# Second scan layer: every state in SBUF, the last columns kept by a DMA, four weight banks in PSUM

## The chip, the cores and the metric

The kernel runs on one core of a Trainium2 chip. The core has a matrix engine (TensorE, "PE" in the profile), a vector engine (VectorE, "DVE"), a scalar engine (ScalarE, "ACT"), GpSimd ("POOL") and SyncE ("SP"), which here only issues DMAs. The engines work through their own queues in order and meet at semaphores. SBUF is the on-chip memory that all of them read and write; PSUM is the small second memory, in eight banks of 512 float32 per partition, which TensorE writes and which VectorE and ScalarE also read and write. GpSimd and the DMAs reach SBUF only here. The metric is the time of one execution on the device, in microseconds.

## The reference

Four layers run one after the other on an image batch of 4 x 96 x 56 x 56: attention, a selective scan in eight directions, window attention, and a selective scan in four directions with a convolutional tail. The change is in the last of them, the second scan layer. Cut to what matters, its scan is

```python
def step(hc, inp):                        # hc: one state per channel d and state index n
    u_t, d_t, B_t, C_t = inp
    hc = hc * jnp.exp(d_t[..., None] * A[None]) + (d_t * u_t)[..., None] * B_t[:, :, None, :]
    return (hc, jnp.einsum('bkdn,bkn->bkd', hc, C_t))
```

with 192 channels, 16 state indices n, 4 directions and a sequence of 56*56 = 3136 positions. For each position the state decays, takes an input, and is summed over n with the weights C.

## The kernel before

All is float32. Two images are worked on together (a "pair"), 64 channels of each on the 128 partitions, so 192 channels are three slices c = 0, 1, 2. The layer runs for two pairs, one after the other. For a pair, `scans` goes over 4 directions times 7 tiles of T = 448 positions, in all 28 **blocks** q. A block has 16 **groups**, one for each n; a group g has three scans (g, c), numbered u = 3g + c. So a pair has 448 groups and 1344 scans. The same function serves both scan layers; `ratio` is true in the second one, and only its branches matter here.

For one group the engines do the following, each in its own queue:

- ACT makes the decay of each scan (L1319, an Exp into `Ar`, a ring of NA = 6) and a weight (L1329, a Tanh into a PSUM bank, a ring of NW = 3 banks, `weight_bank`). The function that orders them makes weight u+2 and decay u+4 in iteration u. Weight u may only be written when the scan that used its bank is over, three scans back (`weight_before`).
- POOL forms du * B for all three slices (`input1`, L1579, into `Tr`, two groups ahead), and multiplies states by C (`project` of POOL, L1595).
- DVE turns a weight into an input in its bank (`input2`, L1454) and runs the scan (`scan`, L1478) with Ar and that bank as its inputs.
- Of every second group (the even ones, `on_dve(g)` = 1 - g % 2) DVE also multiplies slice 0 by C (`project` of DVE, L1485). The state of that slice is written to PSUM bank 3 (`HB`), all other states to SBUF (`Hr`, a ring of NH = 3 groups). POOL's `project` takes the two slices that are left of an even group, and all three of an odd one.
- PE adds the products to a PSUM bank per slice (L1205).
- ACT copies the last column of each state to `st`, from SBUF (`keep_sbuf`, L1340) and from PSUM (`keep_psum`, L1335); 16 groups later `seed` (L1352) puts it in front of the next tile's decays, as the start of that scan. `seed` of group g+1 waits for the last scan of group g-1.
- SP loads B and C of each group, spread over partitions, into `BC` (`spread`, L1638, two DMAs a group, four groups ahead).

DVE's queue for an even group g is: input2, scan (g,0), input2, scan (g,1), project (g,0), input2, scan (g,2). POOL's queue for each group g is: project of g-1, input1 of g+2.

Beside this the next block is prepared: POOL gathers its inputs (L1556, one slice in each of the groups r = 1, 2, 3 of the block) and forms du (L1562, r = 11, 12, 13, the last one when ACT has read `delta` at the start of r = 14); ACT loads another function table and back, with a logarithm between them (r = 9); DVE does `one_less` (L1411, once a block, after scan (10,0)) and three cumulative sums (L1420: after scan (11,2), after (13,0), and after (14,1) just ahead of that group's project).

Of the kernel before, what the change touches and what calls it, by code (L numbers as in the profile page):

```python
# [1028 lines left out]
def scans(chip, K, D, lay, pair, xc, yacc, bcd, S):  # L1029
# [6 lines left out]
    def on_dve(g):  # L1036
        return (1 if ratio else 2) - g % 2
# [4 lines left out]
    def kept_before(g):  # L1042
        return g + (g + 1) // 2 if ratio else 2 * g

    FIRST_SB = 0 if ratio else 1
    NBS = 5 if ratio else 6
    HB, YB, XB = (3, 4, 7) if ratio else (2, 4, 7)
    NA, NW = (6, 3) if ratio else (2, 0)
    TW, TP = T + 1, T + 4
# [19 lines left out]
    with ExitStack() as ctx:  # L1069
# [31 lines left out]
        w_done, t2_done = sems("w_done"), sems("t2_done")  # L1101
        st_done, y_free, merged = sems("st_done"), sems("y_free"), sems("merged")

        def weight_bank(u):
# [16 lines left out]
        def state_at(g, c, first):  # L1121
            return PS[:, HB + c, first:TW] if c < on_dve(g) else Hr[:, g % NH, c - FIRST_SB, first:TW]

# [107 lines left out]
        def act(e):  # L1231
# [110 lines left out]
            def seed(g):  # L1342
# [3 lines left out]
                if g >= ring:  # L1346
                    e.wait_ge(s_done, 3 * (g - ring + 1))
                if q % NT:
                    e.wait_ge(st_done, kept_before(g - 15))
                else:  # L1350
                    e.wait_ge(zeroed, 1)
# [20 lines left out]
            for u in range(-2, NU):  # L1372
# [12 lines left out]
                if c == 0 and g + 1 < NG:  # L1385
                    seed(g + 1)
                if c == 2:
                    keep_sbuf(g)
# [4 lines left out]
                if q + 1 < NQS:  # L1393
                    prepare(q + 1, s)
                if c == 1 and ratio and on_dve(g):
                    keep_psum(g)
            for c in range(3):
                merge(NQS - 1, c)

        def dve(e):  # L1400
# [56 lines left out]
            def scan(g, c):  # L1457
# [10 lines left out]
                else:  # L1468
                    e.wait_ge(t_done, g + 1)
                if c < on_dve(g) and g:  # L1470
                    e.wait_ge(h_done, products_before(g))
                    last = g - 2 if ratio else g - 1
                    if last >= 0:
                        e.wait_ge(st_done, kept_before(last) + 1)
                elif c >= on_dve(g) and g >= NH:
                    e.wait_ge(hp_done, g - NH + 1)
                    e.wait_ge(st_done, kept_before(g - NH + 1))
# [135 lines left out]
        def sp(e):  # L1613
# [14 lines left out]
            def spread(g):  # L1628
# [8 lines left out]
                for m in range(2):  # L1637
                    e.dma_start(BC[64 * m:64 * m + 64, g % NBS],  # L1638
                                bcd[q % 2, 16 * m + nn:16 * m + nn + 1].broadcast_to([64, 2, T])).then_inc(bc_ld[g % NBS], 16)

            put_rows(0)
            for g in range(min(NBS - 1, NG)):
                spread(g)
            for g in range(NG):
# [5 lines left out]
                if g + NBS - 1 < NG:  # L1650
                    spread(g + NBS - 1)

        chip.stage(pe, act, dve, pool, sp)
# [1384 lines left out]
```

## Time and profile before

| | us |
|---|---|
| median of 3 runs | 15305.25 (15288.34 to 15307.01) |
| the profiled execution | 15302.04 |
| its span, first to last instruction | 15299.9 |
| DVE busy over the span | 14142.6 |
| POOL busy over the span | 12419.2 |
| ACT busy over the span | 11996.8 |

The span and the time differ by 2.1 us, so the trace holds the whole of the time. The busy times are over all four layers; what bounds the second scan layer has to be read from its own stretch, which lies at 9838 to 12205 us for the first pair and at 12632 to 15002 us for the second. Instructions of one engine overlap a little in the records: the next starts some 0.09 us before the end shown for the one ahead, so a cost in a queue is read from start to start.

### The profile page before, as it was taken

What the parts mean: (1) busy time and instruction counts of PE and PEld (TensorE: products, weight loads), DVE (VectorE), ACT (ScalarE), POOL (GpSimd) and SP (SyncE); (2) the same over time, 40 slices, a digit from 0 to 9 for tenths busy, and PEclk for the clock granted to TensorE, in tenths of its full rate; (3) what the DMA queues carried; (4) which work ended last, traced back from release to release, by engine and by line L of the source; (5) the groups of instructions that cost most, each with busy time, mean ns of one, the idle gap of its engine ahead of it and who ended that gap; (6) DMA issues with size and microseconds to landing.
All of it is one profiled execution on the core that took longest, in us unless ns stands there. A gap on an engine that the chain in (4) does not pass through costs nothing. (4 is left out here: it accounts for less than half of the span.)

```text
span 15299.9 us, 186073 instructions
## 1 busy us (share of the span) xinstructions
PE 13023.2 (85%) x37976; PEld 5684.4 (37%) x37976; DVE 14142.6 (92%) x19364; ACT 11996.8 (78%) x26319; POOL 12419.2 (81%) x6712
## 2 busy tenths in 40 slices
PE   9999799999999889999999979877777677777776
PEld 3333244444444334444444435433333233333333
DVE  7778699999999989999999988899999979999998
ACT  6777678788888767878888855699889858988996
POOL 1111599999999879999999972599999859999996
PEclk9999899999999999999999989999999889999988
DMA  2110244444444334444444432233333213332331
GB/s 39 30 26 17 69 121 121 122 121 120 119 120 120 107 108 122 120 122 120 120 120 120 120 105 66 61 90 89 89 88 89 83 46 89 89 89 87 89 88 45
DMA packets 543491, 1416.85 MB, mean 93 GB/s; under 512 B 134802, under 2 KB 191274, under 8 KB 538778
## 3 DMA queue, kind: packets, MB, share of 16 engines
q1 hardware_dynamic: 542342, 1404.94, 32.5%
q14 instruction: 845, 6.92, 0.2%
q8 instruction: 304, 4.98, 0.1%
HBM read 1323.37 MB, written 58.28 MB: 90 GB/s over the span
## 5 line engine op out<-in xcount | busy, mean ns | idle before, releaser
L1205 PE MATMUL PS<-Hc,ident 128*128 128x448 f32 x16128 | 7100.2, 580 | 1452.2 <-POOL Hc L1595 1389.6
L1579 POOL TENSOR_TENSOR Tr<-du,BC 128x1344 f32<-128x1344 f32 x2684 | 6886.8, 2566 | 0.0
L1205 PEld LDWEIGHTS PS<-Hc,ident 128*128 128x128 f32 x16128 | 3091.0, 200 | 5346.3 <-issue 2793.0
L1595 POOL TENSOR_TENSOR Hc<-Hr,BC 128x896 f32<-128x896 f32 (+2 forms) x2688 | 4409.1, 1640 | 199.4 <-DVE Hr L1478 193.3
L1319 ACT ACTIVATE PS<-dl,A 128x448 f32<-128x448 f32 x5376 | 3402.4, 633 | 1009.5 <-DVE Hr L1478 689.3
L1478 DVE TENSOR_TENSOR_SCAN Hr<-PS,Tr 128x449 f32<-128x449 f32 x2688 | 2895.4, 1077 | 4.1 <-ACT PS L1319 3.4
L1478 DVE TENSOR_TENSOR_SCAN PS<-PS,Tr 128x449 f32<-128x449 f32 x2688 | 2837.1, 1077 | 60.8 <-ACT PS L1319 57.9
L1478 DVE TENSOR_TENSOR_SCAN Hr<-Ar,PS 128x449 f32<-128x449 f32 x2240 | 2417.2, 1079 | 0.0
L1329 ACT ACTIVATE PS<-cs,lneps,A 128x448 f32<-128x448 f32 x2688 | 1928.5, 719 | 138.2 <-DVE Hr L1478 75.0
L1485 DVE TENSOR_TENSOR Hc<-PS,BC 128x448 f32<-128x448 f32 x3136 | 1823.5, 605 | 0.0
L1454 DVE SCALAR_TENSOR_TENSOR PS<-PS,Tr 128x448 f32<-128x448 f32 x2688 | 1651.7, 614 | 154.9 <-ACT PS L1329 146.3
L1319 ACT ACTIVATE Ar<-dl,A 128x448 f32<-128x448 f32 x2688 | 1764.8, 657 | 0.0
L528 DVE TENSOR_REDUCE mx<-PS 128x1 f32<-128x448 f32 (+1 forms) x2100 | 1204.5, 618 | 328.0 <-PE PS L308 327.0
L494 ACT ACTIVATE Pr<-PS 128x896 f32<-128x896 f32 (+1 forms) x1092 | 936.1, 885 | 403.5 <-PE PS L326 388.3
L620 POOL TENSOR_TENSOR ost<-ost,rb 96x448 f32<-96x448 f32 x84 | 95.0, 1131 | 1313.9 <-DMA rb<-rows 1313.9
L1214 PE MATMUL PS<-yacc,ident 128*128 128x448 f32 (+15 forms) x1320 | 761.0, 685 | 11.3 <-ACT yacc L1310 10.3
L308 PE MATMUL PS<-K,Q 96*128 96x448 bf16 (+1 forms) x2100 | 741.2, 360 | 5.8 <-DMA K<-part 5.5
L326 PE MATMUL PS<-Q,K 99*128 99x448 bf16 (+1 forms) x2100 | 734.0, 358 | 1.4 <-ACT Q L455 0.8
L1335 ACT ACTIVATE st<-PS 128x2 f32<-128x2 f32 (+1 forms) x2240 | 360.6, 161 | 415.8 <-DVE Hc L1485 410.9
L1157 PE MATMUL PS<-dl,ident 128*128 128x448 f32 x984 | 490.7, 582 | 169.7 <-issue 169.7
L1340 ACT ACTIVATE st<-Hr 128x2 f32<-128x2 f32 (+2 forms) x2688 | 519.2, 193 | 76.0 <-DVE Hr L1478 11.0
L340 PE MATMUL PS<-Pr,V 128*32 128x448 f32 (+1 forms) x4200 | 561.7, 551 | 0.0
(288 smaller groups left out, 15088.0 us busy)
## 6 DMA issues: line engine op xcount, KB each, us to landing
BC<-bcscratch SPq DMA_DIRECT2D x5376, 224.0 KB, 3.6
zscratch<-zst SPq DMA_DIRECT2D x84, 224.0 KB, 1.9
bcscratch<-rows SPq DMA_DIRECT2D x336, 56.0 KB, 1.7
z<-zscratch SPq DMA_DIRECT2D x28, 672.0 KB, 4.9
rb<-rows SPq DMA_DIRECT2D x12, 1176.0 KB, 7.1
xg<-mid SPq DMA_DIRECT2D x12, 1176.0 KB, 8.1
xr<-mid SPq DMA_DIRECT2D x56, 168.0 KB, 2.7
rl<-rows SPq DMA_DIRECT2D x56, 168.0 KB, 3.3
```

Source lines behind the costliest of these rows:

```text
L308: e.matmul(PS[0:qn, bank("max", v), 0:T], Q[s][0:96, q0:q0 + qn], KK[s][0:96, i * T:i * T + T], start=True, stop=True).then_inc(full, 1)
L494: e.activation(Pr[0:kn, n % NPR, 0:nt, :], PS[0:kn, 2 * (n % 2):2 * (n % 2) + nt, 0:T], ACT.Exp, scale=scale).then_inc(s_exp, 1)
L528: e.tensor_reduce(mx[0:qn, t, i:i + 1], PS[0:qn, bank("max", v), 0:T], AX.X, ALU.max).then_inc(drained("max", v)[0], 1)
L1205: e.matmul(PS[:, YB + c, 0:T], K["ident"][:], Hc[:, g % NHC, c, :], start=False, stop=(nn == 15)).then_inc(y_done, 1)
L1214: e.matmul(view(PS[:, YB + c, :], ro, rd), K["ident"][:], view(yacc, c * n + off, dims), start=(i == 0), stop=False)
L1319: e.activation(decay_at(u, 1), dl[:, q % 2, c, :], ACT.Exp, scale=A[:, q // NT, c, nn:nn + 1]).then_inc(a_done, 1)
L1329: e.activation(PS[:, weight_bank(u), 1:TW], cs[:, q % 2, c, :], ACT.Tanh, scale=A2[:, q // NT, c, nn:nn + 1], bias=K["lneps"][:]).then_inc ...
L1454: e.scalar_tensor_tensor(out=p, in0=p, scalar=1.0, in1=Tr[:, g % NTR, c, :], op0=ALU.add, op1=ALU.mult).then_inc(t2_done, 1)
L1478: e.tensor_tensor_scan(state_at(g, c, 0), decay_at(u, 0), input_at(g, c), 1.0 if ratio else 0.0, ALU.mult, ALU.add).then_inc(s_done, 1)
L1485: e.tensor_tensor(Hc[:, g % NHC, c, :], state_at(g, c, 1), BC[:, g % NBS, 1, :], ALU.mult).then_inc(h_done, 1)
L1579: e.tensor_tensor(Tr[:, g % NTR] if ratio else Tr[:, g % NTR, :, 1:TW], du[:, q % 2], b, ALU.mult).then_inc(t_done, 1)
L1595: e.tensor_tensor(Hc[:, g % NHC, m:3], Hr[:, g % NH, m - FIRST_SB:3 - FIRST_SB, 1:TW], c_, ALU.mult).then_inc(hp_done, 1)
```

## The change

In the second scan layer only:

- All scans write their states to SBUF (`Hr`); DVE's `project` of an even group, slice 0, reads its state from there. PSUM bank 3 becomes free and joins the ring of weights (NW = 4).
- ACT's two copies of last columns go. SP issues one DMA per group for it (`keep`), from the last column of the three states to `st`, when the group's last scan is done. It stands behind the `spread` of the same iteration.
- `seed` waits for that DMA of 16 groups before. The first scan of a group waits, before it overwrites a slot of `Hr`, for the DMA and for both engines' products of three groups before.

```diff
@@ kept_before, the rings
-        return g + (g + 1) // 2 if ratio else 2 * g
+        return 2 * g
...
-    NA, NW = (6, 3) if ratio else (2, 0)
+    NA, NW = (6, 4) if ratio else (2, 0)
@@ state_at
-            return PS[:, HB + c, first:TW] if c < on_dve(g) else Hr[:, g % NH, c - FIRST_SB, first:TW]
+            return PS[:, HB + c, first:TW] if c < on_dve(g) and not ratio else Hr[:, g % NH, c - FIRST_SB, first:TW]
@@ act: seed
-                if q % NT:
+                if q % NT and ratio:
+                    e.wait_ge(st_out[(g - 16) % NH], 16 * ((g - 16) // NH + 1))
+                elif q % NT:
                     e.wait_ge(st_done, kept_before(g - 15))
@@ act: the loop over u
-                if c == 2:
+                if c == 2 and not ratio:
                     keep_sbuf(g)
...
-                if c == 1 and ratio and on_dve(g):
-                    keep_psum(g)
@@ dve: scan
-                if c < on_dve(g) and g:
+                if ratio:
+                    if g >= NH and c == 0:
+                        e.wait_ge(h_done, products_before(g - NH + 1))
+                        e.wait_ge(hp_done, g - NH + 1)
+                        e.wait_ge(st_out[g % NH], 16 * (g // NH))
+                elif c < on_dve(g) and g:
                     e.wait_ge(h_done, products_before(g))
-                    last = g - 2 if ratio else g - 1
-                    if last >= 0:
-                        e.wait_ge(st_done, kept_before(last) + 1)
+                    e.wait_ge(st_done, kept_before(g - 1) + 1)
@@ sp
+            def keep(g):
+                e.wait_ge(s_done, 3 * g + 3)
+                e.dma_start(st[:, g % 16, :], Hr[:, g % NH, :, T], allow_slow_non_contiguous=True).then_inc(st_out[g % NH], 16)
...
                     spread(g + NBS - 1)
+                if ratio:
+                    keep(g)
```

On DVE, in the program order of one even and one odd group (the engine's scan is listed under the name SCALAR_TENSOR_TENSOR; `Hc` are the products, `BC` the spread B and C), before:

```order
L1454 SCALAR_TENSOR_TENSOR PS<-PS,Tr 128x448
L1478 SCALAR_TENSOR_TENSOR PS<-Ar,PS 128x449
L1454 SCALAR_TENSOR_TENSOR PS<-PS,Tr 128x448
L1478 SCALAR_TENSOR_TENSOR Hr<-Ar,PS 128x449
L1485 TENSOR_TENSOR Hc<-PS,BC 128x448
L1454 SCALAR_TENSOR_TENSOR PS<-PS,Tr 128x448
L1478 SCALAR_TENSOR_TENSOR Hr<-Ar,PS 128x449
L1454 SCALAR_TENSOR_TENSOR PS<-PS,Tr 128x448
L1478 SCALAR_TENSOR_TENSOR Hr<-Ar,PS 128x449
L1454 SCALAR_TENSOR_TENSOR PS<-PS,Tr 128x448
L1478 SCALAR_TENSOR_TENSOR Hr<-Ar,PS 128x449
L1454 SCALAR_TENSOR_TENSOR PS<-PS,Tr 128x448
```

and after:

```order
L1455 SCALAR_TENSOR_TENSOR PS<-PS,Tr 128x448
L1482 SCALAR_TENSOR_TENSOR Hr<-Ar,PS 128x449
L1455 SCALAR_TENSOR_TENSOR PS<-PS,Tr 128x448
L1482 SCALAR_TENSOR_TENSOR Hr<-Ar,PS 128x449
L1489 TENSOR_TENSOR Hc<-Hr,BC 128x448
L1455 SCALAR_TENSOR_TENSOR PS<-PS,Tr 128x448
L1482 SCALAR_TENSOR_TENSOR Hr<-Ar,PS 128x449
L1455 SCALAR_TENSOR_TENSOR PS<-PS,Tr 128x448
L1482 SCALAR_TENSOR_TENSOR Hr<-Ar,PS 128x449
L1455 SCALAR_TENSOR_TENSOR PS<-PS,Tr 128x448
L1482 SCALAR_TENSOR_TENSOR Hr<-Ar,PS 128x449
L1455 SCALAR_TENSOR_TENSOR PS<-PS,Tr 128x448
```

The number of instructions is the same. The project's first input has moved from PSUM to SBUF, so that both of its inputs (Hr and BC) are now in SBUF; that of each scan's output has moved too.

On ACT, two groups in a block (L1329 or L1330 is a weight, L1319 or L1320 a decay, L1352 or L1355 the seed, L1282 or L1283 the copy of `delta` at r = 12, 13 or 14), before:

```order
L1329 ACTIVATE PS<-cs,lneps,A_464 128x448
L1319 ACTIVATE Ar<-dl,A 128x448
L1340 ACTIVATE st<-Hr 128x3
L1329 ACTIVATE PS<-cs,lneps,A_464 128x448
L1319 ACTIVATE Ar<-dl,A 128x448
L1352 ACTIVATE Ar<-still 128x3
L1329 ACTIVATE PS<-cs,lneps,A_464 128x448
L1319 ACTIVATE Ar<-dl,A 128x448
L1335 ACTIVATE st<-PS 128x1
L1329 ACTIVATE PS<-cs,lneps,A_464 128x448
L1319 ACTIVATE Ar<-dl,A 128x448
L1340 ACTIVATE st<-Hr 128x2
```

and after:

```order
L1330 ACTIVATE PS<-cs,lneps,A_470 128x448
L1320 ACTIVATE Ar<-dl,A 128x448
L1330 ACTIVATE PS<-cs,lneps,A_470 128x448
L1320 ACTIVATE Ar<-dl,A 128x448
L1355 ACTIVATE Ar<-still 128x3
L1330 ACTIVATE PS<-cs,lneps,A_470 128x448
L1320 ACTIVATE Ar<-dl,A 128x448
L1330 ACTIVATE PS<-cs,lneps,A_470 128x448
L1320 ACTIVATE Ar<-dl,A 128x448
```

The three copies to `st` of two groups have gone; all else stands in its old order.

On SP, the start of the layer's loop for a pair (L1626 or L1630 writes B and C of a block out, L1618 and L1619 or their successors load the next direction's weights), before:

```order
L1626 DMA bcscratch<-rows 32x448 x2
L1638 DMA BC<-bcscratch 64x896 x8
L1618 DMA xp<-in_l3xp 128x228
L1619 DMA dw<-in_l3dw 12x384
L1638 DMA BC<-bcscratch 64x896 x8
L1626 DMA bcscratch<-rows 32x448 x2
```

and after:

```order
L1630 DMA bcscratch<-rows 32x448 x2
L1642 DMA BC<-bcscratch 64x896 x8
L1622 DMA xp<-in_l3xp 128x228
L1623 DMA dw<-in_l3dw 12x384
L1642 DMA BC<-bcscratch 64x896 x2
L1648 DMA st<-Hr 128x3x1
L1642 DMA BC<-bcscratch 64x896 x2
L1648 DMA st<-Hr 128x3x1
L1642 DMA BC<-bcscratch 64x896 x2
```

The loads of a block stood together; now every pair of loads is followed by the DMA of a group's last columns, 128 partitions x 3 single elements, 896 such DMAs in all.

## Rows read from the trace of the kernel before

**Rows 1.** Busy time of each engine in the first pair of the layer

```profile
9840.00:12205.00 2365.00, 1785.31 (x3820) 760.51 (x3820) 2290.03 (x3017) 2127.03 (x4310) 2215.51 (x1056) 0.91 0.31 88
```

**Rows 2.** One_less, once a block, in two stretches: min/median/max ns, first and last start

```profile
L1411 DVE TENSOR_SCALAR w<-du x12: 1539/1541/1542, 9972.5 to 10899.1; 128x1344 f32<-128x1344 f32 x12
...
L1411 DVE TENSOR_SCALAR w<-du x12: 1539/1540/1543, 11071.3 to 12009.8; 128x1344 f32<-128x1344 f32 x12
```

**Rows 3.** Groups in 11100 to 12100: count, busy us, mean ns, idle before

```profile
L1454 DVE SCALAR_TENSOR_TENSOR PS<-PS,Tr 128x448 f32<-128x448 f32 x564 | 346.6, 615 | 37.6 <-ACT PS L1329 35.8
L1556 POOL COPY xs<-xc 128x448 f32<-128x448 f32 x36 | 36.6, 1017 | 0.0
L1420 DVE TENSOR_TENSOR_SCAN cs<-one,cs,PS 128x448 f32<-128x448 f32 x30 | 33.7, 1122 | 0.0
L1562 POOL TENSOR_TENSOR du<-dl,xs 128x448 f32<-128x448 f32 x33 | 32.3, 978 | 33.6 <-ACT dl L1282 33.6
```

**Rows 4.** Who waited for whom in the same stretch: us, times, longest

```profile
ACT st L1335 <- DVE Hc L1485: 37.8, 46, 1.4
POOL Hc L1595 <- DVE Hr L1478: 22.6, 11, 2.1
```

**Rows 5.** POOL's gather in the first half of the first pair

```profile
L1556 POOL COPY xs<-xc x36: 549/559/565, 9932.9 to 10869.8; 128x448 f32<-128x448 f32 x36
```

**Rows 6.** Timeline of DVE in a plain stretch: start us, length us

```profile
13507.08 0.60 DVE L1485 TENSOR_TENSOR Hc<-PS,BC 128x448 f32<-128x448 f32 x1
13507.59 0.62 DVE L1454 SCALAR_TENSOR_TENSOR PS<-PS,Tr 128x448 f32<-128x448 f32 x1
13508.13 1.08 DVE L1478 TENSOR_TENSOR_SCAN Hr<-Ar,PS 128x449 f32<-128x449 f32 x1
...
13509.64 1.08 DVE L1478 TENSOR_TENSOR_SCAN Hr<-Ar,PS 128x449 f32<-128x449 f32 x1
...
13514.19 1.09 DVE L1478 TENSOR_TENSOR_SCAN PS<-Ar,PS 128x449 f32<-128x449 f32 x1
```

**Rows 7.** Timeline of POOL at the same place

```profile
13503.03 2.56 POOL L1579 TENSOR_TENSOR Tr<-du,BC 128x1344 f32<-128x1344 f32 x1
13505.55 2.56 POOL L1595 TENSOR_TENSOR Hc<-Hr,BC 128x1344 f32<-128x1344 f32 x1
13508.07 2.56 POOL L1579 TENSOR_TENSOR Tr<-du,BC 128x1344 f32<-128x1344 f32 x1
13510.60 1.77 POOL L1595 TENSOR_TENSOR Hc<-Hr,BC 128x896 f32<-128x896 f32 x1
13512.33 2.56 POOL L1579 TENSOR_TENSOR Tr<-du,BC 128x1344 f32<-128x1344 f32 x1
```

**Rows 8.** Timeline at one place of the first pair's tail

```profile
12285.21 1.51 POOL L1773 TENSOR_TENSOR yacc<-yacc,z 128x448 f32<-128x448 f32 x1
...
12285.77 1.44 DVE L775 SCALAR_TENSOR_TENSOR acc<-pad,cw,acc 128x448 f32<-128x448 f32 x1
```

**Rows 9.** The same view, 1.5 us later

```profile
12286.68 1.51 POOL L1773 TENSOR_TENSOR yacc<-yacc,z 128x448 f32<-128x448 f32 x1
```

**Rows 10.** Instructions by line: ns min/median/max, first and last start

```profile
L775 DVE SCALAR_TENSOR_TENSOR PS<-pad,cw,PS x624: 687/690/692, 1709.3 to 15277.7; 128x448 f32<-128x448 f32 x156
L775 DVE SCALAR_TENSOR_TENSOR acc<-pad,cw,acc x128: 683/685/1621, 12284.3 to 15163.2; 128x448 f32<-128x448 f32 x128
...
L1684 DVE TENSOR_TENSOR ysum<-ysum,yacc x28: 624/626/1443, 5324.1 to 15075.1; 128x448 f32<-128x448 f32 x28
...
L1485 DVE TENSOR_TENSOR Hc<-PS,BC x3136: 594/606/618, 1811.7 to 14996.1; 128x448 f32<-128x448 f32 x196
...
L1773 POOL TENSOR_TENSOR yacc<-yacc,z x84: 1125/1137/1647, 5347.7 to 15141.9; 128x448 f32<-128x448 f32 x84
```

**Rows 11.** DMA issues: count, KB each, us from issue to landing

```profile
BC<-bcscratch SPq DMA_DIRECT2D x5376, 224.0 KB, 3.6
...
bn<-in_bn SPq DMA_DIRECT2D x4, 6.0 KB, 1.7
```

More of the change, by code:

```diff
@@ L1102, in scans @@
         st_done, y_free, merged = sems("st_done"), sems("y_free"), sems("merged")
+        st_out = [sems("st_out") for _ in range(NH)]
         def weight_bank(u):
@@ L1651, in sp @@
                     spread(g + NBS - 1)
+                if ratio:
+                    keep(g)
+            if ratio:
+                for i in range(NH):
+                    e.wait_ge(st_out[i], 16 * len(range(i, NG, NH)))
         chip.stage(pe, act, dve, pool, sp)
```

## The prediction

> **What bounds the kernel now.** I read the trace's stretch of this layer first. In the first pair DVE is busy for 2290 of 2365 us, POOL for 2216, ACT for 2127 [rows 1]. So DVE sets the time, POOL is 3% behind it, and ACT has a tenth to spare. The length of a block comes from an instruction that stands once in it: twelve starts in 926.6 us make 84.24 us a block in the first half of a pair, where the gathers are short, and 938.5 / 11 = 85.32 us in the second half, where they are long [rows 2].
>
> Then DVE's own work in a block, from start to start. A scan with its input2 takes 1.51 us (13508.13 to 13509.64) and the project 0.51 (13507.08 to 13507.59) [rows 6]. one_less is 1.54 and a cumulative sum 1.12 long [rows 2, 3], each less the overlap of 0.09. That is 48 x 1.51 + 8 x 0.51 + 1.45 + 3 x 1.03 = **81.2 us**. DVE is idle for the rest, 3.0 us of a block in the first half and 4.1 in the second. The wait that ends last there is for ACT's weight: 35.8 of 37.6 us of idle time before input2 in 1000 us [rows 3]. ACT is late although it has time to spare, because it may not run ahead by more than three banks, and stands itself behind the copies of last columns, which wait for DVE (37.8 us in 1000 before the copy from PSUM alone) [rows 4].
>
> POOL's queue runs without a break in a plain stretch: starts at 3.03, 5.55, 8.07, 10.60 and 12.33 us [rows 7], so 2.52 for input1, 2.52 for an odd group's project, 1.73 for an even one's, 9.29 us for two groups, where DVE needs 6 x 1.51 + 0.51 = 9.57. POOL is idle before a project only 11 times in 1000 us [rows 4]. It is as good as always in the middle of an instruction when DVE comes to its project.
>
> **What the change removes.** ACT loses three copies in two groups and the waits before them, and may be a fourth bank ahead. I take all of DVE's wait for weights as gone: -3.0 us a block in the first half, -4.1 in the second. The bounds are nothing and this.
>
> **What it adds on DVE.** DVE's project now reads Hr and BC, both in SBUF; before, one input was in PSUM. This form with PSUM took 594 to 618 ns in all its 3136 uses, POOL busy or not [rows 10]. A project with both inputs in SBUF isn't in the trace, but other DVE instructions of that kind and size are: L1684 takes 624 ns at least and 1443 at most, L775 with acc 683 and 1621, whereas L775 on PSUM never leaves 687 to 692 [rows 10]. The timeline shows what makes the difference. POOL's L1773 runs to 12286.72, DVE's L775 starts at 12285.77 and ends only at 12287.21, 0.49 us after POOL [rows 8]. POOL's next one starts at 12286.68 and is 1.51 long instead of 1.13 [rows 8 to 10]; POOL goes on 0.38 us late. So a DVE instruction with two inputs in SBUF waits for the end of POOL's instruction, POOL is then held for 0.38, and DVE goes on 0.45 after POOL's changeover (0.49, plus 0.05 and less 0.09 of overlaps).
>
> How long this wait can be is not in the rows: POOL's instructions there are 1.13 us long, here up to 2.57. With the longest surplus of rows 8 as a cap (1.44 - 0.63 = 0.81 us) it costs less, with the end of POOL's instruction as the only limit it can be 2.5. I take the latter, since the end of DVE follows POOL's end and no fixed time. The Trainium skill (SBUF — State Buffer, section "SBUF: two separate sides") says that a DVE instruction with two SBUF inputs and a GpSimd instruction which reads SBUF take a shared port pair by an exclusive lock, and that the loser blocks for the whole instruction. By that page the wait has no cap either, and its sum is the one below; by the cap it would be 15,302.
>
> **The walk through a block**, with both queues side by side:
> - *Plain pairs (r = 0, 6, 8).* From one changeover, DVE is back at its project after 0.45 + 9.07 = 9.52. POOL needs 0.38 + 2.52 (input1) + 1.73 + 2.52 + 2.52 = 9.67 to the end of the odd group's project. DVE waits 0.16 and goes in between project and input1.
> - *r = 2 and r = 4.* POOL has one gather more (0.52 from start to start, later 0.97; 0.04 less than the lengths in [rows 3, 5]) and then two: 0.68 and 1.19 in the first half, 1.13 and 2.09 in the second.
> - *r = 10.* one_less stands ahead of it: DVE comes 1.45 later, 1.30 after the changeover, and meets input1: it waits the rest, 1.22. After that POOL is idle until scan (10,2) is over.
> - *r = 12.* POOL took 1.73 + 2.52 + 0.94 for group 11 against DVE's 4.53, so its project of group 11 ends 3.31 after scan (11,2), and input1 5.83. DVE, with a cumulative sum, comes at 1.03 + 3.02 = 4.06: 1.78.
> - *r = 14.* POOL has waited for ACT's `delta` with its third du (33.6 us in 1000 [rows 3]) and is late with its project: DVE, again behind a sum, waits 0.43.
>
> Together 5.8 us a block in the first half and 7.1 in the second. A block becomes 81.2 + 5.8 - 8 x 0.06 = **86.5** (before 84.24) and 81.2 + 7.1 - 0.5 = **87.8** (before 85.32). That is +2.3 and +2.5, 28 blocks of each: +134 us. In the first block of a pair POOL isn't late yet, DVE meets input1 instead of the gap before it, and it costs 7.5 more, twice: +15.
>
> **The rest.** States of slice 0 into SBUF instead of PSUM: a scan takes 1.08 into SBUF and 1.09 into PSUM [rows 6], 0. The wait of scan (g,0) for both products and the DMA of g-3 is covered by two groups, 9 us. SP's DMA waits for the scans of g; behind it stands the spread of g+5, which waits for POOL's project of g anyway and is read 10 us later. A small DMA lands in 1.7 us, the large ones in 3.6 [rows 11]. One whose last dimension is strided becomes one descriptor per element by the Trainium skill (DMA: Bandwidth & Descriptors, section "Rules for kernel authors"); that would be 384 of 4 bytes, and no row here prices them.
>
> Sum: 15302 + 149 = **15,450 us**, 1.0% slower. The profiled execution is 3 us below the median of the runs, which I neglect.
>
> **The rivals.**
> 1. *The gap is missed* (0.25). The plain pairs hang on 0.15 us. If DVE comes later than that, it meets all of input1: from the end of the odd group's last scan POOL has 0.14 + 2.52 + 2.52 = 5.18 until it is free, DVE comes after 3.02, and waits 2.1. POOL is then on time for the next even group, so it repeats. Each plain pair costs 1.95 more, r = 2 and r = 4 some 1.7 and 1.2: 8.8 us a block in the first half. In the second the long gather makes POOL late again, and 5.9 at most are left. All of it: 15450 + 246 + 165 = 15,860; partly: anything from 15,480 on. For it: the margin is small. Against it: POOL's and DVE's times repeat to 0.01 us.
> 2. *No such wait in this place* (0.09). Then only the removal counts, less 0.6 us of a block for ACT's table change: -2.3 us x 56 = -129, 15,170 us, faster. It decides if DVE's project stays at 0.62 us. For it: POOL's instructions here are longer and of another shape than in the rows. Against it: two DVE lines of different kinds suffer it, and POOL's instructions in the rows are products of two SBUF tensors as here.
> 3. *The wait has the cap of 0.81* (0.07). 4.0 and 4.2 us a block: 84.7 and 84.9, against 84.24 and 85.32: 15,302, no change.
> 4. *The new DMA is slow* (0.05). From a landing of 9 us on scan (g,0) waits; 12 us would cost 0.5 to 1 us per group, 15,900 to 16,300.
>
> The likeliest case has 0.52 (its own range 15,390 to 15,540, from the holds of 0.33 to 0.45 and ACT's waits gone by half); 0.02 is left for what I don't see.
>
> **How the numbers follow.** A measurement of this kernel tells about 0.2% (30 us) from no change. Faster: rival 2 and a little, 0.10. Same: rival 3, 0.07. Slower: the rest, 0.83. The range runs from 15,340 to 15,830: it leaves out rivals 2 and 3 and the far ends of 1 and 4, 0.2 together.
>
> **What would show it.** Right: DVE's project at 0.6 to 3 us with a mean near 1.4, short in plain pairs; POOL's instructions behind it 0.38 longer; DVE's idle time before input2 nearly gone; blocks of 86.5 and 87.8. Rival 1: project near 2.7 in most pairs, blocks near 95 and POOL idle 2 us before an even group's project. Rival 2: project at 0.62 throughout. Rival 4: waits of the scans for the DMA. The prediction is wrong if blocks differ from these by more than 1 us, above all if ACT still makes DVE wait.

## The result, and the profile after

The changed kernel takes **15591.28 us** (median of 4 runs, 15558.6 to 15603.27) against 15303.17 us for the kernel before beside it: a ratio of 1.0188, 95% interval 1.0176 to 1.02. It is 288 us slower; 149 were forecast. Its profiled execution takes 15597.3 us, of which the span is 15595.5.

Nearly all of it lies in the two scan loops: 278 of the 295.6 us between the two profiled spans. The first windows are the busy times of the engines in them, in the columns of [rows 1] (us and count for PE, PEld, DVE, ACT, POOL, then granted clock and DMA share):

```profile
9852.90:12351.60 2498.70, 1823.24 (x3820) 767.81 (x3820) 2492.35 (x3019) 2070.24 (x3643) 2289.59 (x1056) 0.90 0.33 84
12781.30:15297.30 2516.00, 1834.53 (x3820) 770.32 (x3820) 2507.66 (x3019) 2070.95 (x3643) 2287.09 (x1056) 0.89 0.33 83
```

The pairs took 2366.8 and 2369.7 us before, so +132 and +146. The layer begins 14.5 us later than before. Nothing is changed ahead of it; in the eleven other kernels below, equal up to there, it begins at 9829 to 9848 us, so most of this is scatter. DVE is busy for 99.7% of the loop, in the same number of instructions. So its instructions have become longer. Which ones, the groups of DVE, POOL and ACT in the stretch from 11100 to 12100 say (count, busy us, mean ns, idle before), beside [rows 3]:

```profile
L1583 POOL TENSOR_TENSOR Tr<-du,BC 128x1344 f32<-128x1344 f32 x178 | 481.3, 2704 | 0.0
L1330 ACT ACTIVATE PS<-cs,lneps,A 128x448 f32<-128x448 f32 x534 | 383.7, 720 | 38.3 <-DVE Hr L1482 37.2
L1455 DVE SCALAR_TENSOR_TENSOR PS<-PS,Tr 128x448 f32<-128x448 f32 x534 | 322.4, 604 | 0.5 <-POOL Tr L1583 0.5
L1489 DVE TENSOR_TENSOR Hc<-Hr,BC 128x448 f32<-128x448 f32 x89 | 144.0, 1618 | 0.0
L1566 POOL TENSOR_TENSOR du<-dl,xs 128x448 f32<-128x448 f32 x33 | 36.5, 1105 | 47.3 <-ACT dl L1283 47.3
L1283 ACT ACTIVATE dl<-PS 128x448 f32<-128x448 f32 x33 | 17.8, 539 | 36.0 <-PE PS L1163 36.0
```

Two readings. DVE's 37.6 us of idle time before input2 [rows 3] are gone (0.5). And its project is 1618 ns long on average, one us more than before. Over the whole trace, by line (min/median/max ns), the form with PSUM of the first scan layer stands beside the new one:

```profile
L1489 DVE TENSOR_TENSOR Hc<-PS,BC x2688: 585/601/616, 1811.5 to 9024.2; 128x448 f32<-128x448 f32 x192
L1489 DVE TENSOR_TENSOR Hc<-Hr,BC x448: 598/1678/2968, 9855.4 to 15291.0; 128x448 f32<-128x448 f32 x150
```

One_less gives the length of a block, as in [rows 2]: (10888.5 - 10000.5) / 10 = 88.8 us where 86.5 were forecast, and 901.3 / 10 = 90.1 where 87.8 were.

```profile
L1412 DVE TENSOR_SCALAR w<-du x11: 1518/1521/1523, 10000.5 to 10888.5; 128x1344 f32<-128x1344 f32 x11
...
L1412 DVE TENSOR_SCALAR w<-du x11: 1519/1520/1522, 11155.9 to 12057.2; 128x1344 f32<-128x1344 f32 x11
```

The 88.8 holds two of the blocks that miss the gap (below); without them the first half has 88.0 a block on average. In the second pair, where six of them lie in the first half, the same line gives 90.1 in either half.

**A plain pair is what was forecast.** The timeline of DVE at r = 0 of a block:

```profile
10302.66 1.07 DVE L1482 TENSOR_TENSOR_SCAN Hr<-Ar,PS 128x449 f32<-128x449 f32 x1
10303.66 0.68 DVE L1489 TENSOR_TENSOR Hc<-Hr,BC 128x448 f32<-128x448 f32 x1
10304.26 0.62 DVE L1455 SCALAR_TENSOR_TENSOR PS<-PS,Tr 128x448 f32<-128x448 f32 x1
```

and of POOL at the same place:

```profile
10301.29 2.56 POOL L1599 TENSOR_TENSOR Hc<-Hr,BC 128x1344 f32<-128x1344 f32 x1
10303.82 2.94 POOL L1583 TENSOR_TENSOR Tr<-du,BC 128x1344 f32<-128x1344 f32 x1
```

DVE comes 0.16 us before POOL's changeover, goes in behind the product, ends at 10304.34 (0.49 us after it), and POOL's input1 is 2.94 us long instead of 2.56.

**The one place that isn't.** At r = 14 the project should have waited 0.43 us. In 49 of the 54 blocks that prepare a next one it is 2.4 to 3.0 long. DVE there, the sum and the project:

```profile
10379.20 1.11 DVE L1421 TENSOR_TENSOR_SCAN cs<-one,cs,PS 128x448 f32<-128x448 f32 x1
10380.24 2.66 DVE L1489 TENSOR_TENSOR Hc<-Hr,BC 128x448 f32<-128x448 f32 x1
```

POOL (in brackets the idle time ahead and what ended it):

```profile
10372.49 2.56 POOL L1583 TENSOR_TENSOR Tr<-du,BC 128x1344 f32<-128x1344 f32 x1
10378.92 0.98 POOL L1566 TENSOR_TENSOR du<-dl,xs 128x448 f32<-128x448 f32 x1 [3.86 <-ACT dl L1283]
10379.86 2.56 POOL L1599 TENSOR_TENSOR Hc<-Hr,BC 128x1344 f32<-128x1344 f32 x1
```

ACT's `delta`:

```profile
10378.30 0.54 ACT L1283 ACTIVATE dl<-PS 128x448 f32<-128x448 f32 x1 [1.80 <-PE PS L1163]
```

and PE's four parts (eight passes) of the third `total`, on which it waits:

```profile
10373.33 0.99 PE L1158 MATMUL PS<-dl,ident 128*128 128x448 f32 x2 [3.84 <-issue]
10374.16 1.11 PE L1159 MATMUL PS<-du,ident 128*128 128x448 f32 x2
10375.07 1.70 PE L1161 MATMUL PS<-w,nident 128*128 128x448 f32 x2
10376.56 1.70 PE L1163 MATMUL PS<-cs,ident 128*128 128x448 f32 x2
```

PE needs 4.94 us for this sum. In three blocks (1, 8 and 36) it needs 3.25, and there the project at r = 14 is 0.98 us long, as forecast. (In ten blocks it takes 6.06 to 6.17. In eight of them DVE's project starts 0.08 us or more after POOL's and is 2.96 long; in blocks 20 and 48 the two start within 0.02 us of each other, DVE's is 0.60 long and POOL's 3.05 instead of 2.56.) The windows of the same place have the granted clock in the third column from the end:

```profile
10370.00:10375.00 5.00, 1.67 (x4) 0.86 (x5) 5.00 (x7) 2.90 (x6) 4.24 (x2) 0.98 0.23 60
10375.00:10380.00 5.00, 5.00 (x11) 2.36 (x9) 5.00 (x7) 3.07 (x7) 1.14 (x3) 0.68 0.16 33
```

Before this sum PE had no matmul for 3.84 us; within it the granted clock falls from 2.4 to 1.2 GHz (0.68 is the mean over 5 us), and its last four passes take 0.75 us each instead of 0.37. So `delta` comes 1.7 us later, POOL begins its project just before DVE comes to its own, and DVE waits nearly the whole of it.

The kernel before had such slow sums in 15 of 54 blocks, the changed one has them in 51, and the pause ahead of the sum was 2.1 us there. In one of its blocks:

```profile
10245.51 1.01 PE L1157 MATMUL PS<-dl,ident 128*128 128x448 f32 x2 [2.11 <-issue]
```

The pause is longer because, by the kernel's own wait, the third sum may start only when DVE has read the second out of their common bank (its cumulative sum), and in DVE's queue the project of r = 12, with its own wait of 1.78 us at the port, now stands between:

```profile
10366.83 2.32 DVE L1489 TENSOR_TENSOR Hc<-Hr,BC 128x448 f32<-128x448 f32 x1
...
10372.12 1.11 DVE L1421 TENSOR_TENSOR_SCAN cs<-one,cs,PS 128x448 f32<-128x448 f32 x1
```

It ends at 10373.23, PE begins at 10373.33. The longer pause isn't all, since the three sums of 3.25 have 3.84 us ahead of them too; what else sets the moment of the fall isn't shown.

**The gap missed.** In eight blocks, beside the first of each pair where it was forecast, the projects at r = 6 and 8 are 2.3 to 2.7 long instead of 0.68. (Blocks 21 and 49, behind the two projects of 0.60, miss it at r = 0: 2.60 and 2.23.) In all eight PE's projection takes 4.76 us, and in no other block of the loop. Block 6 is the first of them. PE's six passes of the projection in block 5 and in block 6:

```profile
10322.26 3.10 PE L1143 MATMUL PS<-xs,xp 128*76 128x448 f32 x6 [0.52 <-POOL xs L1560]
...
10410.49 4.76 PE L1143 MATMUL PS<-xs,xp 128*76 128x448 f32 x6 [1.02 <-POOL xs L1560]
```

What follows on ACT, and then on DVE and POOL:

```profile
10415.37 0.54 ACT L1247 ACTIVATE rows<-PS 76x448 f32<-76x448 f32 x1 [3.62 <-PE PS L1143]
...
10420.13 0.63 DVE L1455 SCALAR_TENSOR_TENSOR PS<-PS,Tr 128x448 f32<-128x448 f32 x1 [0.44 <-ACT PS L1330]
...
10423.39 2.48 DVE L1489 TENSOR_TENSOR Hc<-Hr,BC 128x448 f32<-128x448 f32 x1
...
10422.83 2.57 POOL L1583 TENSOR_TENSOR Tr<-du,BC 128x1344 f32<-128x1344 f32 x1 [0.18 <-issue]
10427.48 1.77 POOL L1599 TENSOR_TENSOR Hc<-Hr,BC 128x896 f32<-128x896 f32 x1 [2.09 <-DVE Hr L1482]
```

The granted clock is 0.50 there (10409 to 10414), ACT stands for 3.6 us, its fourth bank is used up, DVE's project at r = 6 comes 11.62 us after that at r = 4 instead of 10.68, and POOL's input1 is under way by 0.56. POOL then waits 2.09 us for DVE's scan, is on time again, and the next gap is missed as well: rival 1's picture, until one_less at r = 10 breaks it.

**The DMA** costs nothing that shows. The issues by tile (count, KB, us from issue to landing), where [rows 11] had 3.6 for BC:

```profile
BC<-bcscratch SPq DMA_DIRECT2D x5376, 224.0 KB, 3.6
...
st<-Hr SPq DMA_DIRECT2D x896, 1.5 KB, 2.6
```

In the list of waits no scan and no seed waits for it. It makes 400 packets (packets under 512 B rise from 134802 to 493202, by 896 x 400).

### The profile page after: what moved, and what is told of

Read it like the earlier page. It is cut to its first block and busy times, and to the rows that moved or that the text cites. A ratio compares the mean times of both kernels' runs of the same rounds, so it can differ in the third digit from the quotient of the medians.

```text
span 15595.5 us, 184723 instructions
## 1 busy us (share of the span) xinstructions
PE 13127.4 (84%) x37976; PEld 5707.6 (37%) x37976; DVE 14557.0 (93%) x19364; ACT 11877.0 (76%) x24975; POOL 12560.2 (81%) x6712
## 2 busy tenths in 40 slices
DMA packets 901880, 1418.19 MB, mean 91 GB/s; under 512 B 493202, under 2 KB 549674, under 8 KB 897178
## 5 line engine op out<-in xcount | busy, mean ns | idle before, releaser
L1583 POOL TENSOR_TENSOR Tr<-du,BC 128x1344 f32<-128x1344 f32 x2684 | 7001.3, 2609 | 0.2 <-issue 0.2
L1320 ACT ACTIVATE PS<-dl,A 128x448 f32<-128x448 f32 x5376 | 3402.0, 633 | 1014.4 <-DVE Hr L1482 689.2
L1482 DVE TENSOR_TENSOR_SCAN Hr<-Ar,PS 128x449 f32<-128x449 f32 x2688 | 2880.0, 1071 | 0.0
L1330 ACT ACTIVATE PS<-cs,lneps,A 128x448 f32<-128x448 f32 x2688 | 1930.5, 719 | 177.0 <-DVE Hr L1482 171.9
L1320 ACT ACTIVATE Ar<-dl,A 128x448 f32<-128x448 f32 x2688 | 1767.6, 658 | 0.0
L1489 DVE TENSOR_TENSOR Hc<-PS,BC 128x448 f32<-128x448 f32 x2688 | 1545.0, 601 | 0.0
L1489 DVE TENSOR_TENSOR Hc<-Hr,BC 128x448 f32<-128x448 f32 x448 | 716.7, 1600 | 0.0
L1148 PE MATMUL PS<-rows,dw 12*128 12x448 f32 x1008 | 511.5, 588 | 37.1 <-ACT dl L1260 21.1
```

Source lines behind the costliest of these rows:

```text
L1320: e.activation(decay_at(u, 1), dl[:, q % 2, c, :], ACT.Exp, scale=A[:, q // NT, c, nn:nn + 1]).then_inc(a_done, 1)
L1330: e.activation(PS[:, weight_bank(u), 1:TW], cs[:, q % 2, c, :], ACT.Tanh, scale=A2[:, q // NT, c, nn:nn + 1], bias=K["lneps"][:]).then_inc ...
L1482: e.tensor_tensor_scan(state_at(g, c, 0), decay_at(u, 0), input_at(g, c), 1.0 if ratio else 0.0, ALU.mult, ALU.add).then_inc(s_done, 1)
L1489: e.tensor_tensor(Hc[:, g % NHC, c, :], state_at(g, c, 1), BC[:, g % NBS, 1, :], ALU.mult).then_inc(h_done, 1)
L1583: e.tensor_tensor(Tr[:, g % NTR] if ratio else Tr[:, g % NTR, :, 1:TW], du[:, q % 2], b, ALU.mult).then_inc(t_done, 1)
```

## The experiments

The kernel before ran beside every kernel here; its medians are 15301 to 15306 us.

### Is it the port wait? Taken away, and put in alone

**e1, three banks only.** The changed kernel with its ring of weights as before.

```diff
-    NA, NW = (6, 3) if ratio else (2, 0)     # before; changed kernel: (6, 4)
+    NA, NW = (6, 3) if ratio else (2, 0)
```

> The changed kernel with three weight banks instead of four; nothing else differs. If the loss is DVE's project (both inputs in SBUF) waiting for POOL's instruction, DVE has long waits in each pair of groups in which ACT catches up, so the fourth bank is worth little: between 15,580 and 15,640 us, projects as long as in the changed kernel. If the bank itself matters (a rival: reading or writing the freed bank costs something), the time falls towards 15,303.

15649.57 us, ratio 1.0224 (1.0209 to 1.0239), 10 us above the range that I expected. The fourth bank is worth 58 us in the changed kernel. DVE waits for weights little even without it (3.5 us in 1000); the rest goes through the gap: the projects are 1.70 us long on average (1.60 with four banks), since the gap at r = 6 and 8 is missed more often: in 16 blocks beside the first and the last of each pair instead of 8, and in all 16 the projection takes 4.76 us.

**e2, project with its second input in PSUM.** As e1; bank 3, which is free, holds ones, and DVE's project multiplies by them. It leaves out the product with C of slice 0 in the even groups.

```diff
-                e.tensor_tensor(Hc[...], state_at(g, c, 1), BC[:, g % NBS, 1, :], ALU.mult)
+                e.tensor_tensor(Hc[...], state_at(g, c, 1), PS[:, HB, 1:TW], ALU.mult)
```

> As the run with three banks, but DVE's project takes its second input from the freed PSUM bank, filled once with ones, instead of from BC; the product with C of slice 0 of even groups is left out. All states are in SBUF still and the DMA keeps the last columns. Port theory: with one input in SBUF the project takes 0.61 us always, POOL is not held, blocks take 83 to 85 us, and the time is 15,230 to 15,290 us, below the kernel before. Rival (the DMA of last columns, or the new waits for slots of Hr, cost the time): no change against the run with three banks, some 15,590.

15276.03 us, ratio 0.9981 (0.9972 to 0.9991); 373 us less than e1, and the project never leaves its length:

```profile
L1490 DVE TENSOR_TENSOR Hc<-Hr,PS x448: 591/597/603, 9848.0 to 14973.8; 128x448 f32<-128x448 f32 x150
```

**e5, both inputs in SBUF, alone.** The kernel before; only the project's first input is moved, to the state of slice 1 in SBUF (the product of slice 0's own state with C is left out).

```diff
-                e.tensor_tensor(Hc[...], state_at(g, c, 1), BC[:, g % NBS, 1, :], ALU.mult)
+                e.tensor_tensor(Hc[...], Hr[:, g % NH, 1, 1:TW], BC[:, g % NBS, 1, :], ALU.mult)
```

> The kernel before, all of it, except that DVE's project of an even group reads slice 1 of the states (in SBUF) instead of slice 0 (in PSUM), so that both inputs are in SBUF; the product of slice 0 is left out for it. No DMA of columns, three banks, ACT's copies as before. Port theory: the project waits for POOL's instruction, and since ACT keeps DVE late as well, DVE misses the gap between POOL's project and input1 in plain pairs: waits near 2 us in most pairs, 92 to 96 us a block, 15,700 to 15,800 us, worse than the whole change. Rival (it is the sum of the change's other parts): 15,303.

15823.76 us, ratio 1.0338 (1.0324 to 1.0352), 24 us above the range that I expected. The edit costs 518 us. Not all of it is the operand's place: the project now reads what the scan just ahead of it writes, and starts 0.03 us after that scan's end where it started 0.08 before it, 0.11 x 448 = 50 us at most. The projects alone have become longer by 553 us:

```profile
L1487 DVE TENSOR_TENSOR Hc<-Hr,BC x448: 601/1808/2969, 9846.9 to 15521.2; 128x448 f32<-128x448 f32 x150
```

Here every block misses the gap at r = 6 and 8 (2.1 to 2.9 us each), as rival 1 had it; the changed kernel mostly hits it.

### What the change is worth without the port wait

**e4, the DMA without the rest.** The kernel before, but the SBUF columns are kept by SP's DMA; the PSUM state, its copy by ACT and the three banks stay.

```diff
-                if c == 2:
+                if c == 2 and not ratio:
                     keep_sbuf(g)
+            def keep(g):
+                m = on_dve(g)
+                e.wait_ge(s_done, 3 * g + 3)
+                e.dma_start(st[:, g % 16, m:3], Hr[:, g % NH, m:3, T], ...)
```

> The kernel before (slice 0 of even groups in PSUM, three banks), but the last columns of the states in SBUF are kept by a DMA of SP; ACT copies only the column of the PSUM state. Port theory: nothing waits for POOL, ACT saves two copies in two groups and the waits before them, DVE's idle time before input2 falls, 0.6 to 0.9 us a block: 15,250 to 15,280 us. Rival (the DMA is what costs): above 15,303, with the scans waiting for it.

15277.74 us, ratio 0.9983 (0.9973 to 0.9992). 896 such DMAs cost nothing that shows; two of three copies taken from ACT bring 28 us. DVE still waits 36.5 us in 1000 for weights.

**e9 and e10, project with one input.** The changed kernel, with a DVE project that has one tensor input, in SBUF, and a constant in place of C (so the product with C of slice 0 of the even groups is left out); e10 has two operations instead of one.

```diff
+e9               e.tensor_scalar(Hc[...], state_at(g, c, 1), 1.0, None, ALU.mult)
+e10              e.tensor_scalar(Hc[...], state_at(g, c, 1), 1.0, 1.0, ALU.add, ALU.subtract)
```

> The changed kernel with its four banks, except that DVE's project multiplies the state by the constant 1.0 instead of by C, so that it has a single tensor input, in SBUF (the product with C of slice 0 of the even groups is left out). It has about the length of before (one_less, the same form on three times the elements, is 1.52 us). If a DVE instruction with one SBUF input does not wait for POOL, this shows what the four banks and the copies taken from ACT are worth where there is no port wait. My prediction's step (all of DVE's waits for weights go, -3.0 and -4.1 us a block): the project at 0.5 to 0.6 us, DVE idle before input2 under 5 us in 1000, blocks of 81.5 to 82.5 us, 15,130 to 15,190 us. Rival, from the run with three banks and a weight in PSUM (37.8 us of waits in 1000 although ACT had lost its copies): ACT is late because PE and POOL's gathers make it late, a fourth bank covers only part of it, blocks of 83 to 84.5, 15,220 to 15,280 us. If one input waits as two do: project up to 2.6 us, above 15,400.

> The run before showed that my premise was wrong: one_less has two operations (add, subtract) and takes 1.52 us for 1344 elements, 1.13 ns each, in every use; the project with the single operation is 0.37 to 0.45 us for 448, 0.8 ns each, and this faster form waits for POOL too. So the same kernel again (four banks, the copies by a DMA, the product with C of slice 0 of the even groups left out), with the two operations of one_less. If a form at the slower rate doesn't wait: the project at 0.54 to 0.60 us throughout, and the time shows what four banks and the copies taken from ACT are worth without a port wait. My prediction's step (all waits for weights go): DVE idle before input2 under 5 us in 1000, blocks of 81.5 to 82.5, 15,130 to 15,190 us. Rival (ACT is late because PE and POOL's gathers make it late, and a fourth bank covers part of that): blocks of 83 to 84.5, 15,220 to 15,280. If it waits as well: above 15,400, and any reading from SBUF alone would do it, against the always equal 1.52 us of one_less.

15486.33 us (1.0119, 1.0102 to 1.0136) and 15479.38 us (1.0114, 1.0097 to 1.013): both missed the ranges of my step and of its rival, and fell under the third case, that one input waits as two do. Neither gave the number it was for. e9's project, and one_less of the same run:

```profile
L1489 DVE TENSOR_SCALAR Hc<-Hr x448: 368/1409/2795, 9850.8 to 15183.2; 128x448 f32<-128x448 f32 x150
...
L1412 DVE TENSOR_SCALAR w<-du x12: 1521/1521/1522, 9992.8 to 10949.6; 128x1344 f32<-128x1344 f32 x12
```

The shortest takes 0.37 us, 0.82 ns per element, where one_less takes 1.13 ns. So this instruction runs at a higher rate per element, and it waits for POOL with one input as the product does with two. Two operations do not change that (367/1412/2735 in e10). Why one_less keeps to the lower rate, with the same two operations, isn't settled. It reads three slices with gaps between them and the project reads one, but no run changed its tensors.

**e11, four banks, one input in PSUM.** The changed kernel; the project multiplies by what stands in the PSUM bank of the group's third input, which is filled by then and not yet free. It leaves out the product with C of slice 0 in the even groups.

```diff
+                    e.wait_ge(t2_done, 3 * g + 3)
-                e.tensor_tensor(Hc[...], state_at(g, c, 1), BC[:, g % NBS, 1, :], ALU.mult)
+                e.tensor_tensor(Hc[...], state_at(g, c, 1), PS[:, weight_bank(3 * g + 2), 1:TW], ALU.mult)
```

> The two runs before did not give the number that they were for: a project at the fast rate (0.37 us) waits for POOL too, with one operation or two. Here the changed kernel keeps its four banks and its DMA, and DVE's project multiplies the state by what stands in the PSUM bank of the group's third input in place of C (the product with C of slice 0 of the even groups is left out), so that one of its inputs is in PSUM, as before the change. The length should be 0.60 us in every use. The time then is what the change would give with no port wait. By my prediction's step (all of DVE's waits for weights go): DVE idle before input2 under 5 us in 1000, blocks of 81.5 to 82.5 us, 15,130 to 15,190 us. Rival: with three banks and the same freedom ACT still made DVE wait 37.8 us in 1000, so ACT is late because POOL's gathers and PE make it late; a fourth bank covers only part: blocks of 83 to 84.5, 15,220 to 15,280 us.

15231.05 us, ratio 0.9956 (0.994 to 0.9973). The project takes 0.60 us throughout, and one_less gives the blocks, in the first half and in the second:

```profile
L1412 DVE TENSOR_SCALAR w<-du x13: 1521/1525/1548, 9962.7 to 10947.0; 128x1344 f32<-128x1344 f32 x13
...
L1412 DVE TENSOR_SCALAR w<-du x12: 1522/1526/1529, 11117.0 to 12055.5; 128x1344 f32<-128x1344 f32 x12
```

The time is in the rival's range and not in mine. The first half has 984.3 / 12 = 82.0 us a block (84.24 before): nearly every wait gone (DVE waits 3.0 us for weights in 9960 to 10900, before 22.8), as my step had it. The second half has 938.5 / 11 = 85.32 us, to the hundredth what it was before: nothing gained there. (In the second pair's second half it is 84.7 instead of 85.4, a little gained.) The waits of e11 in 11100 to 12100 show why (us, times, longest):

```profile
ACT rows L1247 <- PE PS L1143: 38.8, 11, 3.6
DVE PS L1455 <- ACT PS L1330: 36.2, 70, 1.1
...
PEld PS L1143 <- POOL xs L1563: 26.7, 11, 2.4
```

Where a gather takes 1.02 us and not 0.55, POOL gives PE the gathered slice late, PE the projection, and ACT stands up to 3.6 us in each block before it; in the first half it is 14.0 us in 11 blocks, 1.3 at most. A fourth bank hardly covers the former.

**e8, the gathers earlier.** e4, and the gathers at r = 0, 1, 2 instead of 1, 2, 3, PE's projection a group earlier with them.

```diff
-                if ratio and 1 <= r < 4:
-                    gather(q, r - 1)
+                if ratio and r < 3:
+                    gather(q, r)
-                first = 4 if ratio else 3
+                first = 3
```

> The kernel of the fourth run (PSUM state kept by ACT, SBUF columns by the DMA), with the gathers of the next block on POOL one group earlier (r = 0, 1, 2) and PE's projection and first two delta products as well (r = 3, 4, 5). What is left of DVE's idle time there, 1.3 us a block before scan s = 16 in the second half and 0.2 in the first, comes from ACT waiting for PE, and PE for POOL's gather. If so, it goes: 15,200 to 15,250 us. Rival (ACT's own work is the limit): no change from 15,278.

15243.02 us, ratio 0.9959 (0.9946 to 0.9971): 63 us less than the kernel before, 35 less than e4 and 348 less than the changed one, with the whole computation. DVE's wait for weights in 11100 to 12100 falls from 36.5 us in e4 to 14.2. That fits the chain that e11 shows. But in the second pair (13900 to 14900) it falls only from 37.1 to 29.7, and the blocks stay at 85.3 us there; why isn't shown.

### What made it worse than forecast, and other orders

**e3, a shorter third sum.** The changed kernel; PE leaves out two of the four parts of the third `total` (so slice 2's `delta` is another than the reference's).

```diff
-                e.matmul(X_, K["ident"][:], du[:, s, c, :], start=False, stop=False)
+                if not (ratio and c == 2):
+                    e.matmul(X_, K["ident"][:], du[:, s, c, :], start=False, stop=False)
...
+                if not (ratio and c == 2):
                     e.matmul(X_, K["nident" if ratio else "ident"][:], w1[:, c, :], start=False, stop=False)
```

> The changed kernel, where the third of the three sums that PE makes for the next block's delta leaves out two of its four matmuls (du and w1), so that it takes half as long. In the changed kernel that sum takes 4.94 us in most blocks, when the granted clock falls to 1.2 GHz within it, and 3.25 in three of them; the project of group r = 14 takes 2.68 us in the former and 0.98 in the latter. If the one causes the other (POOL's third du waits for delta, and its project of group 13 is late), the project at r = 14 takes some 0.98 us in all blocks, a block is 1.7 us shorter and the time is 15,480 to 15,530 us. Rival (DVE meets POOL there because of its own phase): 15,590, project unchanged at 2.7.

15483.85 us, ratio 1.0116 (1.0101 to 1.0131), 107 us less than the changed kernel. The project at r = 14 falls from a mean of 2.45 us to 0.92, and the other seven keep their means to 0.02 (0.74 instead of 0.81 at r = 0 apart):

```profile
L1491 DVE TENSOR_TENSOR Hc<-Hr,BC x448: 668/1180/2929, 9831.4 to 15165.4; 128x448 f32<-128x448 f32 x150
```

1.53 x 56 = 86 us are that: the sum's length, with the wait it brings, is the missing piece of the forecast. In the two loops the gain is 99 us; the other 13 are r = 0 (4) and idle time of DVE (14.6 us in the changed kernel, 5.5 in e3). e3 shortens the sum by taking passes away and not by a faster clock; the three blocks with quick sums in the changed kernel (0.98 us) show the same without an edit.

**e6, the project behind the group's first scan.** The changed kernel, with DVE's order (g,0), project, (g,1), (g,2).

> The changed kernel, with DVE's project of an even group moved up one scan, right behind scan (g,0) and what is prepared there. DVE comes to it 1.5 us earlier, when POOL is in the project of the odd group before, and can't miss the gap behind it. Port theory: POOL sets the time in plain pairs (9.67 us for two groups, as before the move), and the waits at r = 10, 12 and 14 change: r = 14 no longer meets a project that just began. 15,400 to 15,520 us. Rival (a wait is a wait wherever the project stands): 15,590.

15581.13 us, ratio 1.0187 (1.0171 to 1.0203), a miss. r = 14 came right (0.78 us), and blocks of the first half in the first pair are 86.0 to 87.3 behind the first two. But r = 0 rose from 0.81 to 1.55 us and r = 10 from 1.61 to 2.24, and in the second half and parts of the second pair the queues settled into another alternation, blocks of 88.7 and then 92.2. Moving the place moves which POOL instruction is met; it doesn't remove the meeting.

**e7, all products on POOL.** The changed kernel without a DVE project.

```diff
-        return (1 if ratio else 2) - g % 2
+        return 0 if ratio else 2 - g % 2
```

> The changed kernel, with all three slices of all products on POOL and none on DVE, so that no DVE instruction of the loop has two inputs in SBUF. POOL then has 4 x 2.52 = 10.08 us in two groups, 80.7 us in a block and 2 to 4 for gathers and du; DVE has 77. Port theory: POOL never is held and sets the time, blocks of 85.5 to 87.5, 15,390 to 15,470 us: slower than before by POOL's own work, but faster than the changed kernel. Rival (POOL's load is what costs in the changed kernel): slower than 15,591.

15403.56 us, ratio 1.0063 (1.0049 to 1.0076), as expected. POOL is the bound now, busy for 2383 of 2410 us in the first pair, DVE idle 100.8 us in 1000 before input2. Even so it beats the port wait by 188 us.

## Why the prediction was right, and where its size was off

**What the number is worth.** 15,591 us lies in the stated range (15,340 to 15,830), but that range took in most of rival 1; the likeliest case alone ended at 15,540. By the prediction's own sign of being wrong, blocks that differ by more than 1 us, it fails: 88.8 and 90.1 are 2.3 us longer than 86.5 and 87.8. The mechanism was found and half of its cost; that the total came out inside is in part the room left for another cause.

**Right: the mechanism and the sign.** DVE's project with two SBUF inputs waits for the end of POOL's instruction, beyond the cap of rival 3, and POOL is held after it. e2 and e5 show it from both sides: -373 us, and +518 of which at most 50 are another wait. e11 shows the sum of all else: without the wait the change gives -70 us, with it +288. So the wait costs 360.

**Right: the walk, seven of its eight terms.** Durations in a typical block of the first half, r = 0 to 12: forecast (wait + 0.54) 0.70, 1.22, 1.73, 0.70, 0.70, 1.76, 2.32, measured (medians of blocks 1 to 13) 0.68, 1.18, 1.68, 0.68, 0.68, 1.74, 2.32; at r = 2 and 4 in the second half 1.64 and 2.60, forecast 1.67 and 2.63. They came from two rows of another part of the kernel [rows 8, 9] and from lengths in POOL's queue. The first block of a pair takes 96.6 us, forecast 94.0.

**The step that failed: "r = 14 ... DVE, again behind a sum, waits 0.43".** It waits 1.9 on average. The durations there are 2.45 instead of 0.97, 1.48 x 56 = 83 us. I had POOL late by what its wait for `delta` was before [rows 3]. That wait depends on DVE's second cumulative sum, which my own term at r = 12 delays by 1.78 us, and then on PE, whose sum takes 4.7 us or more and not 3.25 in 51 of 54 blocks. The walk held DVE and POOL side by side and left PE's sum at its length of before. The kernel before has slow sums too, in 15 blocks; its project doesn't wait for POOL. In the three blocks with a quick sum the forecast for r = 14 is right, 0.98 against 0.97, though their pause is as long: it is the slow sum that failed the term.

**Rival 1 came in part.** The gap is missed at r = 6 and 8 in eight blocks more than forecast, set off by a slow projection of PE (4.76 us instead of 2.5 to 3.1) and not by DVE's or POOL's own times, which do repeat to 0.01 us. The argument against this rival left out PE and ACT. e1 shows the same in 16 blocks. In e5 the gap is missed in every block, in most with a projection of 2.5 to 3.0, so a slow projection isn't the only way to it.

**The account.** 448 projects take 717 us; by the forecast's durations they would take 618: +98 (83 at r = 14; the rest are the missed gaps, less what the last block of each pair saves, which prepares nothing). DVE idle in the loops, taken as 0: +15. That leaves 16 of the 129 us between 278 in the loops and 149. Of these 11 come from counting 28 blocks of 84.24 and 28 of 85.32 us before (4747.7), where the loops took 4736.6; the last 5 I don't place.

**Right, but for half of the reason: ACT's waits.** In the changed kernel they are gone (0.5 us in 1000). e11 shows that the banks and the copies do this only where the gathers are short; in the second half the waits are still there in e11, so in the changed kernel they go because DVE itself stands at the port and ACT catches up. That this term came true in the second half was luck. This didn't move the total, since DVE was to be busy all the time either way; it makes rival 2's time (15,170) too low: without the port wait the change is worth -70 us and not -129.

**Slips in the working.** The terms of DVE's own work add up to 81.1 us and not 81.2, 6 us less in the total. Rival 2's -2.3 us a block doesn't follow from its terms: -3.0 and -4.1, less 0.6, are -2.95 on average, -165 us. And rival 3's cap of 0.81 was already exceeded in [rows 10], where L775 with acc takes 1621 ns against 685.

**Right: the DMA is hidden, states into SBUF cost nothing that shows** (e4 for the one; e2, and scans of 1.07 us, for the other).

## What to carry to other kernels

Before a result is moved from PSUM to SBUF, look at who reads it next: a VectorE product that keeps one input in PSUM is free of GpSimd, and the same product with both in SBUF waits for whatever GpSimd is in the middle of, here 1.0 us on average for an instruction of 0.6. With both engines nearly full, walk their queues side by side; the waits came out to 0.05 us that way, but only where a third engine's lateness was in the walk too. And a wait for a weight isn't cured by more buffers alone when the engine that makes it is itself kept waiting further up: the fourth bank brought 45 us (e11 against e2), mostly in the first halves, and moving the three gathers a group earlier brought 35 with three banks (e8 against e4). No run has both.

## What the runs showed of the hardware

- **The wait at the port lasts until POOL's instruction ends.** No shorter cap is seen: the project is up to 2.97 us long instead of 0.60, behind POOL instructions of 2.56; POOL's next one is held for 0.38 us (2.94 for 2.56) by the product, and for 0.15 (2.71) by the one-input form.
- **One input is enough, at the higher rate.** A tensor-scalar from SBUF to SBUF at 0.82 ns per element (0.37 us) waits as the product does, up to 2.8 us; one_less at 1.13 ns per element takes 1518 to 1552 ns in all its uses in the changed kernel. The Trainium skill (SBUF — State Buffer, section "SBUF: two separate sides") names both cases, a DVE operation in a 2-port mode and one with two SBUF inputs against a GpSimd operation that reads SBUF. e5 agrees with the second; e9 fits the first, if its higher rate is such a mode, which no row names.
- **The granted clock reaches engines that never touch PE.** A dip to 1.2 GHz in a PE that is busy for 73% of the loop makes a sum of eight passes 1.7 us longer (4.94 instead of 3.25), and by ACT and POOL DVE's project at r = 14 2.4 us or more instead of 0.98 in 49 of 54 blocks.
- **A DMA of 384 single elements of 4 bytes** lands in 2.6 us; 896 of them leave the landing of the 224 KB loads beside them at 3.6.
